# A graph kernel's edge tables: the source's one-hot factored into a row of 128 and a tile

## The chip, the cores and the metric

The kernel runs on one core of a Trainium2 chip. The time is that of the device, in microseconds (us), as the median of three runs. A profile is one further execution with the hardware profiler on.

## What is computed

A graph with 1250 nodes and 21250 edges, sorted by destination; node features are 1250 x 512 in f32. Four layers of attention along the edges with a small MLP each, then one weighted aggregation along the same edges:

```
scores = einsum('ehd,ehd->eh', q[src], k[dst]);  attn = softmax of scores over the edges of each src
out    = segment_sum(attn * v[dst], src)                       # 4 layers, 4 heads
msgs   = x[dst] * edge_weight[:, None]
x      = layernorm(x + segment_sum(msgs, src) @ weight.T)      # last step
```

The kernel replaces the sparse steps by dense ones. It first makes two tables of 1250 x 1250: how often an edge goes from node s to node d (its logarithm is added to dense scores), and the sum of the edge weights for each such pair (the matrix of the last step).

## The kernel before

The stage that matters is the making of the two tables (CW, 128 rows x 2 tables x 10 source tiles x 1250 destinations, f32 in SBUF). The source node is the row: node s lies in tile s // 128, row s % 128. Edges are cut into 56 groups (NG) of 3 x 128 (GK = 3 blocks b); an edge of a block is one row of the matmul's contraction. As the edges are sorted by destination, all of a group lie in a window of 28 destinations (WIN) that begins at a base read from a table. If a group broke that rule, a general path would be taken by a flag; it isn't here.

For each group n:

- VectorE (sources, L1054) and ScalarE (L797) make one-hots of the edges' source over all 1280 places: VectorE one block of three, and a second in one group of four, in bf16; ScalarE the others in fp8.
- VectorE (window, L1047) compares the destination's offset with 28 places, for four groups at once (a chunk); GpSimd (weigh, L611) multiplies that mask with three bf16 parts of the edge weight. This gives 4 x 28 = 112 columns per block: a count and three weight parts.
- TensorE (L1575 to L1581) makes 10 tiles x 3 blocks = 30 matmuls, the one-hot of 128 sources as the loaded operand, the 112 columns as the moving one, into three PSUM banks; groups alternate between two sets of banks.
- VectorE (groups, L1075) adds four slices of 10 x 28 into CW: the counts, and one after the other the three weight parts.

The order in each engine is written out by hand. One-hots are made three groups ahead (AHEAD = 3, four buffers). TensorE's group n waits for VectorE's additions of group n-2. In between, each engine does other early work at fixed groups: on VectorE the angles of the conditioning (before group 8), residuals of rows (before groups 16 and 24) and statistics of x (before group 48); on ScalarE sines, SiLU and casts; on TensorE the conditioning's matmuls. Before the first group a plan is made: the edge lists are loaded as 56 x 384, cast by ScalarE (L740, L742), reduced to each group's base on VectorE (L1014 to L1018), turned by TensorE (turn_edges, L1506) and copied to eT (L1021). The semaphore eplan tells that it is there. At the same time GpSimd, ScalarE and the DMA queue fill CW with zeros. The stage ends with the memset at L1161 (tables_done); the layers wait for it.

Of the kernel before, what the change touches and what calls it, by code (L numbers as in the profile page):

```python
# [46 lines left out]
SLOT = 128  # L47
CHUNK_G = 4
NCH = NG // CHUNK_G
SBUFS = 4  # L50
AHEAD = SBUFS - 1
UNROLL_G = 2 * CHUNK_G
# [34 lines left out]

BOTH = 0
# [52 lines left out]
def build(nc, T, out):  # L141
    ctx = ExitStack()
    with ctx:
# [79 lines left out]
        with ExitStack() as prep:  # L223
            rest_of_weights = sb("rest_of_weights", [P, V_HEAD], F32, prep)
            with ExitStack() as load:
                iota_i = sb("iota_i", [P, NP], I32, load)
                src_i = sb("src_i", [NG, GE], I32, load)
                dst_i = sb("dst_i", [NG, GE], I32, load)
                ef = sb("ef", [NG, 4, GE], F32, load)
                gcol = sb("gcol", [NG, 2], F32, load)  # L230
            with ExitStack() as full:
                oh_src = sb("oh_src", [P, P], BF16, full)
                oh_dst = sb("oh_dst", [P, 4, N], BF16, full)
            onehot = sb("onehot", [P, SBUFS, 2, NP], BF16, prep)
            oh8 = sb("oh8", [P, SBUFS, 2, NP], F8, prep)
# [14 lines left out]
        with ExitStack() as start_of_layer:  # L250
            wv_hi = sb("wv_hi", [P, KT, D], F32R, start_of_layer)
            with ExitStack() as prep:
                wv_raw = sb("wv_raw", [P, KT, D], F32, prep)
            wv_lo = sb("wv_lo", [P, KT, D], F32R, start_of_layer)
            with ExitStack() as prep:
                eT = sb("eT", [P, 4, GK, NG], F32, prep)
                wpart = sb("wpart", [P, 3, NG, GK], BF16, prep)
# [10 lines left out]
        with ExitStack() as prep:  # L268
            wres = sb("wres", [P, GK, NG], F32, prep)
            win = sb("win", [P, 2, CHUNK_G * GK, 4, WIN], BF16, prep)  # L270
# [34 lines left out]
        e_win, e_parts, e_onehot, e_sum, e_count, e_chain = (sem(n) for n in ("e_win", "e_parts", "e_onehot", "e_sum", "e_count", "e_chain"))  # L305
# [16 lines left out]
        counted_groups = [e_sum, e_chain, e_count, g_chain, a_onehot]  # L322
# [229 lines left out]
        def _(pool):  # L552
# [55 lines left out]
            between = {8: (cond_rest,), 10: (last_x,)}  # L608

            pool.wait_ge(eplan, 2)  # L610
            def weigh(c, lo, hi):  # L611
                for part in range(3):
                    oh = win[:, c % 2, lo * GK:hi * GK, 0, :].rearrange("p (g b) w -> p g b w", b=GK)
                    o = win[:, c % 2, lo * GK:hi * GK, 1 + part, :].rearrange("p (g b) w -> p g b w", b=GK)
                    wp = wpart[:, part, c * CHUNK_G + lo:c * CHUNK_G + hi, :]
                    m = pool.tensor_tensor(o, oh, wp.unsqueeze(3).to_broadcast([P, hi - lo, GK, WIN]), ALU.mult)
                m.then_inc(e_parts, 1)

            pool.wait_ge(e_win, 1)
            weigh(0, 0, 1)  # L620
            weigh(0, 1, CHUNK_G)
            flag = pool.value_load(grow_i[0:1, NG:NG + 1], min_val=0, max_val=1)
            for c in range(NCH):
                if c:
                    with pool.If(flag < 1):
                        pool.wait_ge(e_win, c + 1)
                        weigh(c, 0, CHUNK_G)
                        pool.wait_ge(e_parts, c + 2)
                for work in between.get(c, ()):
                    work()  # L630
# [101 lines left out]
        def _(act):  # L732
# [58 lines left out]
            with act.If(flag < 1):  # L791
                for n in range(NG):
# [205 lines left out]
        def _(dve):  # L998
# [13 lines left out]

            dve.wait_ge(dst_cast, 1)
# [3 lines left out]
            dve.wait_ge(off_made, 1)  # L1017
            dve.tensor_reduce(gcol[:, 1:2], ef[:, 1, :], AX.X, ALU.max).then_inc(off_made, 1)  # L1018
# [12 lines left out]
            turned(0, 0)  # L1031
            link(dve.tensor_tensor(wres[:], weight, parts[0], ALU.subtract))
            link(dve.tensor_copy(parts[1], wres[:]))
            dve.wait_ge(edges_turned, 3)
            turned(1, 2)
            link(dve.tensor_tensor(wres[:], wres[:], parts[1], ALU.subtract))
            dve.tensor_copy(grow[:].rearrange("o k g -> o (k g)"), ps[0:1, 2 * 512 + cols:2 * 512 + cols + 2 * NG])
            link(dve.tensor_copy(parts[2], wres[:]))
            dve.tensor_scalar(near[:], eT[:, 0, :, 0:NG], -STEP, NEAR, ALU.mult, ALU.add)
            turned(2, 3).then_inc(eplan, 1)  # L1040
# [6 lines left out]
            def window(c, first):  # L1047
                off = eT[:, 1, :, first].rearrange("p b g -> p g b")
                dve.tensor_tensor(win[:, c, :, 0, :].rearrange("p (g b) w -> p g b w", b=GK),
                                  iota_h[:, 0:WIN].unsqueeze(1).unsqueeze(1).to_broadcast([P, CHUNK_G, GK, WIN]),  # L1050
                                  off.unsqueeze(3).to_broadcast([P, CHUNK_G, GK, WIN]), ALU.is_equal)\
                   .then_inc(e_win, 1)

            def sources(j, b, group):  # L1054
                m = dve.tensor_scalar(onehot[:, j % SBUFS, b, :], iota_h[:], eT[:, 0, b, group], HOT, ALU.is_equal, ALU.mult)  # L1055
                if b == (1 if j % CHUNK_G == BOTH else 0):
                    m.then_inc(e_onehot, 1)

            window(0, slice(0, CHUNK_G))
# [15 lines left out]
            def groups(i):  # L1075
                for j in range(UNROLL_G):
                    dve.wait_ge(e_sum, START + i * UNROLL_G + j + 1)
                    base = dve.value_load(grow_i[0:1, bass.ds(i * UNROLL_G + j, 1)], min_val=0, max_val=N - WIN)  # L1078
                    sums = ps[:, (j % 2) * 3 * 512:(j % 2) * 3 * 512 + NT * SLOT].rearrange("p (t s) -> p t s", s=SLOT)
                    sums = sums[:, :, 0:4 * WIN].rearrange("p t (k w) -> p k t w", k=4)  # L1080
                    counts = CW[:, 0, :, bass.ds(base, WIN)]
                    weights = CW[:, 1, :, bass.ds(base, WIN)]
                    at = START + i * 3 * UNROLL_G + 3 * j
                    ahead = bass.ds(i * UNROLL_G + j + AHEAD, 1)
                    dve.wait_ge(e_chain, at)
                    dve.tensor_tensor(weights, weights, sums[:, 1], ALU.add).then_inc(e_chain, 1)  # L1086
                    dve.wait_ge(e_count, START + i * UNROLL_G + j)
                    dve.tensor_tensor(counts, counts, sums[:, 0], ALU.add).then_inc(e_count, 1)  # L1088
                    dve.wait_ge(e_chain, at + 1)
                    dve.tensor_tensor(weights, weights, sums[:, 2], ALU.add).then_inc(e_chain, 1)  # L1090
                    if i * UNROLL_G + j + AHEAD < NG:
                        sources(j + AHEAD, 0, ahead)
                    dve.wait_ge(e_chain, at + 2)
                    dve.tensor_tensor(weights, weights, sums[:, 3], ALU.add).then_inc(e_chain, 1)  # L1094
                    if i * UNROLL_G + j + AHEAD < NG:
                        if (j + AHEAD) % CHUNK_G == BOTH:
                            sources(j + AHEAD, 1, ahead)
                    if j == 0:
                        window(1, bass.ds(i * UNROLL_G + CHUNK_G, CHUNK_G))
                    if j == CHUNK_G and (i + 1) * UNROLL_G < NG:  # L1100
                        window(0, bass.ds(i * UNROLL_G + UNROLL_G, CHUNK_G))
# [34 lines left out]
            with dve.If(flag < 1):  # L1136
                groups(NG // UNROLL_G - 1)
                dve.wait_ge(e_chain, START + 3 * NG)
                dve.wait_ge(e_count, START + NG)
# [352 lines left out]
        def _(pe):  # L1492
# [21 lines left out]
            pe.wait_ge(src_cast, 1)  # L1514
            turn_edges(0, 0).then_inc(edges_turned, 1)
            pe.wait_ge(dst_cast, 1)
            turn_edges(2, 3)
            pe.wait_ge(off_made, 1)
            turn_edges(1, 2)
            pe.wait_ge(off_made, 2)  # L1520
# [3 lines left out]
            m.then_inc(edges_turned, 1)  # L1524

# [36 lines left out]
            for n in range(NG):  # L1562
                for work in between.get(n, ()):
                    work()
                with pe.If(flag < 1):
                    c, gl = divmod(n, CHUNK_G)
                    if gl == 0:
                        pe.wait_ge(e_parts, c + (2 if c else 1))
                    elif n == 1:
                        pe.wait_ge(e_parts, 2)  # L1570
                    pe.wait_ge(e_onehot, n + 1)
                    pe.wait_ge(a_onehot, START + n + 1)
                    pe.wait_ge(e_chain, START + 3 * (n - 1))
# [399 lines left out]
```

## Time and profile before

| | us |
|---|---|
| median of 3 runs | 1860.27 |
| lowest and highest | 1858.53, 1863.58 |
| the profiled execution | 1858.52 |
| its span in the profile | 1856.7 |

The profile's page gives each engine's busy time, and the span in 40 slices of 46.4 us, each digit a tenth of busy time. The table stage is in the first four slices.

```profile
PE 1745.5 (94%) x11805; PEld 1500.2 (81%) x11805; DVE 1245.1 (67%) x2366; ACT 908.2 (49%) x1468; POOL 432.3 (23%) x545
PE   4766999999999999999999999999999999999998
DVE  7898865675856567668665665677557657675844
ACT  9996454454542445445433554455335446453221
POOL 3233130010381301001743010005621001036201
PEclk9998999999999999999999999999999999999899
```

PE is TensorE's matmuls, PEld its loads of the left operand, DVE VectorE, ACT ScalarE, POOL GpSimd. PEclk is the granted clock of TensorE in tenths of full speed. L1494 is the helper through which all matmuls go.

### The profile page before, as it was taken

To read this page: it belongs to the slowest core of one execution; us is meant where nothing else is said; L and a number is where in the kernel's file an instruction comes from. 1 tells how busy PE (TensorE), PEld (TensorE's weight loads), DVE (VectorE), ACT (ScalarE), POOL (GpSimd) and SP (SyncE) were. 2 spreads that over 40 slices of the span, in tenths; PEclk is the share of its full clock that TensorE was granted. 3 is DMA by queue.
4 is the path that set the end of the run, shared out by engine and by line. 5 is a ranking of instruction groups with operands and counts; after the bars stand their busy time and mean duration, and the time that the engine had idled before them with its cause. 6 is when DMAs were issued, how large, how long until landed. Compare 5 with 4: busy or idle time off the path is not lost.

```text
span 1856.7 us, 30729 instructions
## 1 busy us (share of the span) xinstructions
PE 1745.5 (94%) x11805; PEld 1500.2 (81%) x11805; DVE 1245.1 (67%) x2366; ACT 908.2 (49%) x1468; POOL 432.3 (23%) x545
## 2 busy tenths in 40 slices
PE   4766999999999999999999999999999999999998
PEld 4665778888887888888888888887888888879777
DVE  7898865675856567668665665677557657675844
ACT  9996454454542445445433554455335446453221
POOL 3233130010381301001743010005621001036201
PEclk9998999999999999999999999999999999999899
DMA  3041552242310324224201332332114224241121
GB/s 126 2 130 69 209 160 89 95 129 89 114 39 22 105 76 142 95 75 132 67 23 59 108 125 81 106 116 75 35 30 131 87 82 146 85 139 43 42 89 64
DMA packets 63885, 168.62 MB, mean 91 GB/s; under 512 B 5957, under 2 KB 24250, under 8 KB 63735
## 3 DMA queue, kind: packets, MB, share of 16 engines
q10 hardware_dynamic: 23040, 102.41, 16.9%
q1 hardware_dynamic: 40700, 64.25, 10.8%
q8 instruction: 95, 1.56, 0.3%
q14 instruction: 50, 0.41, 0.1%
HBM read 145.04 MB, written 16.99 MB: 87 GB/s over the span
## 4 chain that ended last, share of the span: by engine, by line
PE 79%; DVE 10%; issue 4%; ACT 2%; DMA 1%; POOL 1%; DVEq 1%; SPq 0%; ACTq 0%; POOLq 0%
PE ps L1494 68%; PE ps L1716 9%; PE ps L1635 2%; DVE onehot L1055 1%; DVE prob L1248 1%; DVE CW L1088 1%; DVE PT_lo L1264 1%; DVE CW L1090 1%; DVE CW L1094 1%; POOL x L657 1%; DVE CW L1086 1%; ACT PT_hi L865 1%; DMA piece<-in_L_gnn_m_w_dram 1%; PE ps L1933 1%; DVEq L1078 0%
## 5 line engine op out<-in xcount | busy, mean ns | idle before, releaser
L865 ACT ACTIVATE PT_hi<-ps 128x512 fp32r<-128x512 f32 x400 | 238.4, 596 | 246.3 <-PE ps L1716 246.1
L1264 DVE TENSOR_TENSOR PT_lo<-ps,PT_hi 128x512 fp32r<-128x512 f32 x400 | 274.4, 687 | 49.8 <-ACT PT_hi L865 42.3
L847 ACT ACTIVATE prob<-prob,nmax 128x1250 f32<-128x1250 f32 x160 | 214.2, 1339 | 136.8 <-DVE nmax L1248 136.8
L1716 PE MATMUL ps<-ident,prob 128*128 128x128 f32 x1600 | 248.2, 278 | 12.2 <-DVE PT_lo L1264 12.0
L1248 DVE CUSTOM_DVE_ANT_0 prob<-ps,Lr 128x1250 f32<-128x1250 f32 x160 | 232.4, 1452 | 31.9 <-PE ps L1494 30.6
L1716 PEld LDWEIGHTS ps<-ident,prob 128*128 128x128 f32 x1600 | 181.9, 140 | 78.7 <-DVE PT_lo L1264 61.5
L1494 PE MATMUL ps<-PT_hi,v_hi 128*128 128x256 f32 x800 | 228.2, 285 | 1.2 <-DVE PT_lo L1264 1.2
L1494 PE MATMUL ps<-PT_lo,v_hi 128*128 128x256 f32 x800 | 226.1, 283 | 0.0
L1494 PE MATMUL ps<-PT_hi,v_lo 128*128 128x256 f32 x800 | 225.6, 282 | 0.0
L1494 PE MATMUL ps<-yT,wqk_hi 128*128 128x512 f32 (+1 forms) x768 | 213.0, 364 | 0.0
L1494 PE MATMUL ps<-k_hi,q_hi 128*128 128x512 f32 (+2 forms) x480 | 191.8, 400 | 0.5
L1494 PE MATMUL ps<-k_hi,q_lo 128*128 128x512 f32 (+2 forms) x480 | 169.7, 353 | 0.0
L1494 PE MATMUL ps<-k_lo,q_hi 128*128 128x512 f32 (+2 forms) x480 | 169.5, 353 | 0.0
L653 POOL TENSOR_TENSOR wo_lo<-piece,wo_hi 128x512 fp32r<-128x512 f32 x16 | 20.4, 1273 | 613.8 <-ACT wo_hi L896 613.8
L1494 PEld LDWEIGHTS ps<-PT_hi,v_hi 128*128 128x128 f32 x800 | 152.4, 191 | 2.5 <-issue 2.0
L1494 PEld LDWEIGHTS ps<-PT_lo,v_hi 128*128 128x128 f32 x800 | 152.7, 191 | 0.1
L1494 PEld LDWEIGHTS ps<-PT_hi,v_lo 128*128 128x128 f32 x800 | 152.6, 191 | 0.0
L1278 DVE SCALAR_TENSOR_TENSOR x<-ps,rnorm,x 128x512 f32<-128x512 f32 x160 | 119.3, 746 | 47.2 <-PE ps L1494 47.2
L1494 PE MATMUL ps<-win,onehot 128*128 128x112 bf16 x700 | 94.1, 222 | 59.3 <-DVE CW L1094 46.1
L1494 PEld LDWEIGHTS ps<-yT,wqk_hi 128*128 128x128 f32 x768 | 132.1, 189 | 19.2
L1494 PE MATMUL ps<-yT,wqk_lo 128*128 128x512 f32 (+1 forms) x384 | 137.1, 357 | 0.0
L797 ACT ACTIVATE oh<-iota_h,near 128x1280 fp8e4<-128x1280 f16 x98 | 125.1, 1350 | 7.7 <-PE ps L1494 7.6
(210 smaller groups left out, 3790.9 us busy)
## 6 DMA issues: line engine op xcount, KB each, us to landing
Lr<-l_table ACTq DMA_DIRECT2D x160, 625.0 KB, 3.9
piece<-in_L_gnn_m_w_dram SPq DMA_DIRECT2D x32, 256.0 KB, 2.7
w_table<-CW SPq DMA_DIRECT2D x5, 1250.0 KB, 8.2
prob<-w_table SPq DMA_DIRECT2D x10, 625.0 KB, 4.0
x<-in_x_dram SPq DMA_DIRECT2D x2, 2304.0 KB
CW<-CW SPq DMA_DIRECT2D x7, 625.0 KB
piece<-in_L_gnn_wo_dram SPq DMA_DIRECT2D x16, 256.0 KB, 4.8
piece<-in_L_gnn_wq_dram SPq DMA_DIRECT2D x15, 256.0 KB, 2.8
```

The costliest lines, as they stand in the source:

```text
L653: pool.tensor_tensor(lo, raw, hi.bitcast(F32), ALU.subtract).then_inc(S["piece_split"], 1)
L657: pool.tensor_tensor(x[:, t, :], x[:, t, :], bo_rows[:], ALU.add).then_inc(S["bo_added"], 1)
L797: m = act.activation(oh8[:, n % SBUFS, b - 1, :], iota_h[:], ACT.Abs_reciprocal_sqrt, bias=near[:, b, n:n + 1], scale=STEP, saturate=False)
L847: act.activation(buf, buf, ACT.Exp, bias=nmax[:, i % 4:i % 4 + 1], scale=-1.0, accum_out=prob[:, i % 3, N:N + 1]).then_inc(S["exped"], 1)
L865: act.activation(o, i, ACT.Copy).then_inc(S["pt_hi"], 1)
L1055: m = dve.tensor_scalar(onehot[:, j % SBUFS, b, :], iota_h[:], eT[:, 0, b, group], HOT, ALU.is_equal, ALU.mult)
L1248: dve.tensor_tensor_reduce(prob[:, i % 3, 0:N], ps[:, off:off + N], Lr[:, i % LBUFS, :], -1.0, BIG, ALU.add, ALU.min, nmax[:, i % 4:i % 4 ...
L1264: dve.tensor_tensor(lo, i, hi.bitcast(F32), ALU.subtract).then_inc(S["pt_split"], 1)
L1278: dve.scalar_tensor_tensor(out=x[:, t, :], in0=bank(wo_bank(h, t)), scalar=rnorm[:, i % 8:i % 8 + 1], in1=x[:, t, :], op0=ALU.mult, op1=AL ...
L1494: return pe.matmul(o, a, b, start=start, stop=stop)
L1635: m = pe.transpose(bank(5 + n % 2, k * P, (k + 1) * P), y[:, k * P:(k + 1) * P], ident[:])
L1716: m = pe.transpose(bank(5 + n % 2, at * P, (at + 1) * P), prob[:, (NT * h + 2 * g + j) % 3, d * P:(d + 1) * P], ident[:])
```

## The change

The source's one-hot over 1280 places is split into two factors. A node's row (s % 128) becomes a one-hot of 128, made four times per block on VectorE: plain, and times the weight, the weight's remainder after its first bf16 part, and the remainder after two (each rounded to bf16 as it is written). These are the loaded operands (left). The node's tile and the destination's offset become one place, tile x 28 + offset, of 280; its one-hot is made by ScalarE in fp8 for all three blocks (right), and is the moving operand. TensorE makes 12 matmuls of 280 columns into two banks per group. VectorE adds both tables in one operation. GpSimd's products, the window masks and the semaphores e_win, e_parts and e_count go. The tile is found by scaling and rounding in the plan (rows_made), the place is made after the offsets. The wpart, source and destination copies, needed by the general path alone, come after the first three groups' rows. Buffers are laid out anew: ef has 6 parts, iota_i, src_i and others no longer share memory with the general path's.

```diff
 @@ VectorE, the plan @@
+            dve.wait_ge(src_cast, 1)
+            link(dve.tensor_scalar(ef[:, 5, :], ef[:, 0, :], 1.0 / P, -(P - 1.0) / (2 * P), ALU.mult, ALU.add))
+            link(dve.tensor_scalar(ef[:, 5, :], ef[:, 5, :], MAGIC, None, ALU.add))
+            link(dve.tensor_scalar(ef[:, 5, :], ef[:, 5, :], -MAGIC, None, ALU.add))
+            dve.scalar_tensor_tensor(out=ef[:, 4, :], in0=ef[:, 5, :], scalar=-float(P), in1=ef[:, 0, :], op0=ALU.mult, op1=ALU.add)\
+               .then_inc(rows_made, 1)
             dve.wait_ge(dst_cast, 1)
...
             dve.wait_ge(off_made, 1)
+            dve.wait_ge(rows_made, 1)
+            dve.scalar_tensor_tensor(out=ef[:, 5, :], in0=ef[:, 5, :], scalar=float(WIN), in1=ef[:, 1, :], op0=ALU.mult, op1=ALU.add)\
+               .then_inc(off_made, 1)
...
-            def sources(j, b, group):
-                m = dve.tensor_scalar(onehot[:, j % SBUFS, b, :], iota_h[:], eT[:, 0, b, group], HOT, ALU.is_equal, ALU.mult)
...
+            def rows(j, group):
+                for b in range(GK):
+                    for part in range(4):
+                        weight = (None, eT[:, 3, b, group], wres[:, 0, b, group], wres[:, 1, b, group])[part]
+                        m = dve.tensor_scalar(left[:, j % SBUFS, b, part, :], iota_h[:, 0:P], eT[:, 4, b, group], weight,
+                                              ALU.is_equal, ALU.mult if part else ALU.bypass)
+                m.then_inc(e_onehot, 1)
+
             for j in range(AHEAD):
-                for b in range(2 if j % CHUNK_G == BOTH else 1):
-                    sources(j, b, slice(j, j + 1))
+                rows(j, slice(j, j + 1))
+            dve.wait_ge(edges_turned, 4)
+            turned(0, 4)
+            turned(2, 5)
+            dve.tensor_copy(parts[2], wres[:, 1])
...
 @@ VectorE, one group @@
-                    dve.tensor_tensor(weights, weights, sums[:, 1], ALU.add).then_inc(e_chain, 1)
...
-                    dve.tensor_tensor(counts, counts, sums[:, 0], ALU.add).then_inc(e_count, 1)
...
+                    sums = ps[:, (j % 2) * 1024:(j % 2) * 1024 + 1024].rearrange("p (k s) -> p k s", k=2)[:, :, 0:PLACES]
+                    both = CW[:, :, :, bass.ds(base, WIN)]
+                    dve.wait_ge(e_chain, START + i * UNROLL_G + j)
+                    dve.tensor_tensor(both, both, sums.rearrange("p k (t w) -> p k t w", w=WIN), ALU.add).then_inc(e_chain, 1)
                     if i * UNROLL_G + j + AHEAD < NG:
+                        rows(j + AHEAD, bass.ds(i * UNROLL_G + j + AHEAD, 1))
 @@ ScalarE @@
-                    for b in (2,) if n % CHUNK_G == BOTH else (1, 2):
-                        m = act.activation(oh8[:, n % SBUFS, b - 1, :], iota_h[:], ACT.Abs_reciprocal_sqrt, bias=near[:, b, n:n + 1], scale=STEP,
-                                           saturate=False)
+                    for b in range(GK):
+                        m = act.activation(right[:, n % SBUFS, b, :], iota_h[:, 0:PLACES], ACT.Abs_reciprocal_sqrt, bias=near[:, b, n:n + 1],
+                                           scale=STEP, saturate=False)
 @@ TensorE @@
+                    if n >= 2:
+                        pe.wait_ge(e_chain, START + n - 1)
+                    at = (n % 2) * 1024
+                    for b in range(GK):
+                        for part in range(4):
+                            o = ps[:, at:at + PLACES] if part == 0 else ps[:, at + 512:at + 512 + PLACES]
+                            m = mm(o, left[:, n % SBUFS, b, part, :], right[:, n % SBUFS, b, :],
+                                   b == 0 and part < 2, b == GK - 1 and part in (0, 3))
```

## Rows read from the trace of the kernel before

**Rows 1.** Busy time by stage: stretch, length, busy us of each engine, clock, DMA share, GB/s.

```profile
21.24:177.01 155.77, 103.00 (x1703) 93.88 (x1700) 139.30 (x326) 138.25 (x119) 38.28 (x56) 0.95 0.17 44
```

**Rows 2.** Groups by line: op, shapes, count, busy us, mean ns, idle before.

```profile
L797 ACT ACTIVATE oh<-iota_h,near 128x1280 fp8e4<-128x1280 f16 x98 | 125.1, 1350 | 7.7 <-PE ps L1494 7.6
L1055 DVE TENSOR_SCALAR onehot<-iota_h,eT 128x1280 bf16<-128x1280 f16 x70 | 44.1, 634 | 0.0
L1086 DVE TENSOR_TENSOR CW<-CW,ps 128x280 f32 x56 | 24.8, 443 | 21.7 <-PE ps L1494 12.1 <-DVE CW L1094 8.0 <-issue 1.4
L1264 DVE TENSOR_TENSOR PT_lo<-ps,PT_hi 128x512 fp32r<-128x512 f32 x400 | 274.4, 687 | 49.8 <-ACT PT_hi L865 42.3
```

**Rows 3.** Waits from 21 to 177 us: total us, times, longest.

```profile
PE ps L1494 <- DVE CW L1094: 46.8, 44, 7.2
DVE CW L1086 <- PE ps L1494: 12.1, 5, 6.5
DVE CW L1086 <- DVE CW L1094: 8.0, 22, 0.7
```

**Rows 4.** Tensor_scalar by line and shape; the last gives minimum, median, maximum in ns.

```profile
L1111 DVE TENSOR_SCALAR sin_b<-sin_b 128x640 f32<-128x640 f32 x1 | 0.5, 495 | 0.0
L1110 DVE TENSOR_SCALAR sin_b<-sin_b,fcol 128x640 f32<-128x640 f32 x1 | 0.6, 553 | 0.0
L1468 DVE TENSOR_SCALAR res<-x,mv,rs 128x512 f32<-128x512 f32 x10 | 5.5, 547 | 9.9 <-POOL rs L728 9.9
L1039 DVE TENSOR_SCALAR near<-eT 128x168 f32<-128x168 f32 x1 | 0.2, 249 | 0.0
L1055 DVE TENSOR_SCALAR onehot<-iota_h,eT x70: 541/547/901, 12.6 to 169.0; 128x1280 bf16<-128x1280 f16 x70
```

**Rows 5.** VectorE in order of time: start, duration in us, line, idle before.

```profile
24.62 0.90 DVE L1055 TENSOR_SCALAR onehot<-iota_h,eT 128x1280 bf16<-128x1280 f16 x1
...
60.57 0.45 DVE L1086 TENSOR_TENSOR CW<-CW,ps 128x280 f32 x1 [0.35 <-issue]
...
61.65 0.55 DVE L1055 TENSOR_SCALAR onehot<-iota_h,eT 128x1280 bf16<-128x1280 f16 x1
62.11 0.44 DVE L1094 TENSOR_TENSOR CW<-CW,ps 128x280 f32 x1
```

**Rows 6.** VectorE in order of time, in the last part.

```profile
1736.36 0.51 DVE L1430 TENSOR_SCALAR x<-x,mv,rs 128x512 f32<-128x512 f32 x1
1736.79 0.68 DVE L1425 TENSOR_TENSOR x<-x 128x512 f32<-128x512 f32 x1
```

**Rows 7.** The chain that ended last, TensorE's first group.

```profile
17.48 2.97 PE ps L1494 x30
```

**Rows 8.** VectorE in order of time, around the other work in the stage.

```profile
40.23 0.15 DVE L1107 TENSOR_SCALAR fcol<-fcol_i 128x1 f32<-128x1 int32 x1
...
47.21 0.45 DVE L1086 TENSOR_TENSOR CW<-CW,ps 128x280 f32 x1 [0.37 <-issue]
...
67.12 2.28 DVE L1120 TENSOR_TENSOR row_raw<-row_raw,row_part 69x2048 f32<-69x2048 f32 x1
...
152.25 0.69 DVE L1071 BATCH_NORM_STATS2 bn<-x 128x6 f32<-128x512 f32 x1
...
157.00 0.45 DVE L1086 TENSOR_TENSOR CW<-CW,ps 128x280 f32 x1 [0.67 <-issue]
...
177.01 0.06 DVE L1161 MEMSET viol<- 1x1 f32 x1 [0.62 <-DVE CW L1094]
```

**Rows 9.** VectorE and ScalarE in order of time, at the start.

```profile
6.32 1.16 DVE L1016 TENSOR_SCALAR ef<-ef,gcol 56x384 f32<-56x384 f32 x1
...
12.57 2.15 DVE L1055 TENSOR_SCALAR onehot<-iota_h,eT 128x1280 bf16<-128x1280 f16 x4
14.62 1.28 ACT L797 ACT_TABLE_LOAD   x1
21.24 0.45 DVE L1086 TENSOR_TENSOR CW<-CW,ps 128x280 f32 x1 [6.52 <-PE ps L1494]
```

More of the change, by code:

```diff
@@ L46 @@
 WIN = 28
-SLOT = 128
-CHUNK_G = 4
-NCH = NG // CHUNK_G
+PLACES = NT * WIN
 SBUFS = 4
 AHEAD = SBUFS - 1
-UNROLL_G = 2 * CHUNK_G
+UNROLL_G = 8
 ET = NG * GK
@@ L86 @@
 HALF = NP // 2
-BOTH = 0
 HOT = 2.0 ** -6
@@ L225, in build @@
             with ExitStack() as load:
[L226 to L235, printed above, removed]
+                oh_src = sb("oh_src", [P, P], BF16, load)
+                oh_dst = sb("oh_dst", [P, 4, N], BF16, load)
+            iota_i = sb("iota_i", [P, NP], I32, prep)
+            src_i = sb("src_i", [NG, GE], I32, prep)
+            dst_i = sb("dst_i", [NG, GE], I32, prep)
+            ef = sb("ef", [NG, 6, GE], F32, prep)
+            gcol = sb("gcol", [NG, 2], F32, prep)
+            left = sb("left", [P, SBUFS, GK, 4, P], BF16, prep)
             grow = sb("grow", [1, 2, NG], F32, prep)
@@ L268, in build @@
         with ExitStack() as prep:
-            wres = sb("wres", [P, GK, NG], F32, prep)
-            win = sb("win", [P, 2, CHUNK_G * GK, 4, WIN], BF16, prep)
+            wres = sb("wres", [P, 2, GK, NG], F32, prep)
+            wpart = sb("wpart", [P, 3, NG, GK], BF16, prep)
+            right = sb("right", [P, SBUFS, GK, PLACES], F8, prep)
+            after_right = sb("after_right", [P, 80], F32, prep)
             after_y1 = sb("after_y1", [P, 24], F32, prep)
@@ L304, in build @@
         a_onehot = sem("a_onehot")
-        e_win, e_parts, e_onehot, e_sum, e_count, e_chain = (sem(n) for n in ("e_win", "e_parts", "e_onehot", "e_sum", "e_count", "e_chain"))
+        e_onehot, e_sum, e_chain, rows_made = (sem(n) for n in ("e_onehot", "e_sum", "e_chain", "rows_made"))
         g_chain, g_onehot, g_sum = (sem(n) for n in ("g_chain", "g_onehot", "g_sum"))
@@ L606, in last_x @@
                 pool.memset(x[:, NT - 1, :], 0.0).then_inc(f_set, 1)
[L608 to L630, printed above, removed]
+            cond_rest()
+            last_x()
             pool.wait_ge(bias_copied, 1)
@@ L1030, in _ @@
             dve.wait_ge(edges_turned, 2)
-            turned(0, 0)
-            link(dve.tensor_tensor(wres[:], weight, parts[0], ALU.subtract))
-            link(dve.tensor_copy(parts[1], wres[:]))
+            turned(4, 0)
+            link(dve.tensor_tensor(wres[:, 0], weight, parts[0], ALU.subtract))
+            link(dve.tensor_copy(parts[1], wres[:, 0]))
+            link(dve.tensor_tensor(wres[:, 1], wres[:, 0], parts[1], ALU.subtract))
             dve.wait_ge(edges_turned, 3)
[L1035 to L1040, printed above, removed]
+            link(turned(5, 2))
+            dve.tensor_scalar(near[:], eT[:, 5, :, 0:NG], -STEP, NEAR, ALU.mult, ALU.add).then_inc(eplan, 1)
+            link(dve.tensor_copy(grow[:].rearrange("o k g -> o (k g)"), ps[0:1, 2 * 512 + cols:2 * 512 + cols + 2 * NG]))
             link(dve.tensor_reduce(viol[:], grow[:, 1, :], AX.X, ALU.max))
@@ L1078, in groups @@
                     base = dve.value_load(grow_i[0:1, bass.ds(i * UNROLL_G + j, 1)], min_val=0, max_val=N - WIN)
[L1079 to L1085, printed above, removed]
-                    dve.tensor_tensor(weights, weights, sums[:, 1], ALU.add).then_inc(e_chain, 1)
-                    dve.wait_ge(e_count, START + i * UNROLL_G + j)
-                    dve.tensor_tensor(counts, counts, sums[:, 0], ALU.add).then_inc(e_count, 1)
-                    dve.wait_ge(e_chain, at + 1)
-                    dve.tensor_tensor(weights, weights, sums[:, 2], ALU.add).then_inc(e_chain, 1)
-                    if i * UNROLL_G + j + AHEAD < NG:
[L1092 to L1101, printed above, removed]
+                    sums = ps[:, (j % 2) * 1024:(j % 2) * 1024 + 1024].rearrange("p (k s) -> p k s", k=2)[:, :, 0:PLACES]
+                    both = CW[:, :, :, bass.ds(base, WIN)]
+                    dve.wait_ge(e_chain, START + i * UNROLL_G + j)
+                    dve.tensor_tensor(both, both, sums.rearrange("p k (t w) -> p k t w", w=WIN), ALU.add).then_inc(e_chain, 1)
+                    if i * UNROLL_G + j + AHEAD < NG:
+                        rows(j + AHEAD, bass.ds(i * UNROLL_G + j + AHEAD, 1))
             def angles():
@@ L1513, in _ @@
             turn_edges(3, 1).then_inc(edges_turned, 1)
[L1514 to L1520, printed above, removed]
+            pe.wait_ge(rows_made, 1)
+            turn_edges(4, 0).then_inc(edges_turned, 1)
+            pe.wait_ge(off_made, 3)
+            turn_edges(5, 2)
             for i in range(2):
@@ L1524, in _ @@
             m.then_inc(edges_turned, 1)
+            turn_edges(0, 4)
+            turn_edges(2, 5).then_inc(edges_turned, 1)
             def turn_biases():
@@ L1565, in _ @@
                 with pe.If(flag < 1):
[L1566 to L1570, printed above, removed]
                     pe.wait_ge(e_onehot, n + 1)
                     pe.wait_ge(a_onehot, START + n + 1)
-                    pe.wait_ge(e_chain, START + 3 * (n - 1))
-                    pe.wait_ge(e_count, START + n - 1)
-                    for s in range(NT):
-                        for b in range(GK):
-                            at = (n % 2) * 3 * 512 + s * SLOT
-                            by_act = b == 2 or b == 1 and n % CHUNK_G != BOTH
-                            m = mm(ps[:, at:at + 4 * WIN], oh8[:, n % SBUFS, b - 1, nt(s)] if by_act else onehot[:, n % SBUFS, b, nt(s)],
-                                   win[:, c % 2, gl * GK + b].rearrange("p k w -> p (k w)"), b == 0, b == GK - 1)
+                    if n >= 2:
[6 more added lines that the diff above has]
+                                   b == 0 and part < 2, b == GK - 1 and part in (0, 3))
                     m.then_inc(e_sum, 1)
             with pe.If(flag < 1):
-                pe.wait_ge(e_chain, START + 3 * (NG - 1))
-                pe.wait_ge(e_count, START + NG - 1)
+                pe.wait_ge(e_chain, START + NG - 1)
             with pe.Else():
```

17 lines of the change are left out of this document (3 added, 14 removed).

## The prediction

> **What bounds the kernel now.** I read the busy times by stage first, to see where the change can act at all. The table stage runs from the first addition into the tables at 21.24 us to the small memset at 177.01 us that releases the layers; that is 155.77 us, in which VectorE is busy for 139.3 and ScalarE for 138.3, TensorE for 103 at a mean granted clock of 0.95, and GpSimd for 38 [rows 1]. Everything behind it is untouched by the diff, and nothing of it can begin before that memset, so the forecast is the change in length of this stage and in its start.
>
> Next come the groups by line [rows 2]. ScalarE makes 98 one-hot tiles of 1280 columns at 1.35 us each, VectorE 70 at 0.63 us, and VectorE adds four slices of 280 columns for each of the 56 groups, 0.44 us apiece. The reader is to see that neither engine has much idle time: two engines share the bound. The waits say the same [rows 3]: TensorE stands 46.8 us behind VectorE's fourth addition, and VectorE 12.1 us behind TensorE and 8.0 us behind its own chain. So VectorE's 139.3 busy us of 155.8 are the floor of this stage. Relief for ScalarE alone could give back at most the rest, 16.5 us, and only while VectorE's own work does not grow. VectorE's work is therefore what has to be priced.
>
> **What a short VectorE operation costs.** The change replaces long operations with many short ones, so the fixed part decides. Durations first [rows 4]. A tensor_scalar on f32 without a per-partition operand takes 249 ns for 168 columns and 495 for 640: (495-249)/(640-168) = 0.52 ns a column, and 162 ns that do not depend on width. With one per-partition operand the 640 columns take 553 ns: 58 ns for the operand. With two, 512 columns take 547 ns; 162 + 2x58 + 512x0.52 = 544. So each operand is paid for, one after the other. The one-hot of 1280 columns, f16 to bf16 with one operand, has a median of 547 ns; less 162 and 58 leaves 0.256 ns a column, half of what f32 takes.
>
> What counts in a row of operations is not the duration but the spacing of the starts. In the steady stretch the one-hot starts at 61.65 and the next addition at 62.11: 0.46 us for a duration of 0.55, so 0.09 is overlapped [rows 5]. A one-hot of 128 columns with one operand is then spaced by 162 + 58 + 33 - 90 = 0.16 us. With two operands it is 0.22 by the same sum. The one spacing of a two-operand operation that I found gives less: 1736.36 to 1736.79 is 0.43 for 512 columns [rows 6], less 0.266 of streaming plus 0.033 is 0.197. I take 0.205, between the ends 0.197 and 0.22 and nearer to the measured spacing.
>
> **The change, part by part.**
>
> *Rows (VectorE).* Each group gets 12 operations of 128 columns: three with one operand (the plain one-hot) and nine with two (place and weight): 3x0.16 + 9x0.205 = 2.325 us. Three groups are made ahead, 53 in the loop.
>
> *Additions (VectorE).* One of 2x280 columns for four of 280. A tensor_tensor takes 443 ns for 280 columns and 687 for 512, 1.05 ns a column [rows 2]: 443 + 280x1.05 = 737 ns, less 0.09 of overlap 0.65 us. Four cost 4x(0.443-0.09) = 1.41, so this part saves 0.76 us a group. It also ends the chain wait of 8.0 us [rows 3], since 12 operations now lie between two additions.
>
> *Removed from VectorE:* 70 long one-hots (44.1 us busy) and the window masks. Some of the former are slowed while GpSimd weighs the masks, 0.90 us for 0.55 at 24.62 [rows 5]; with GpSimd's products gone (most of its 38 busy us in this stage) I price every short operation undisturbed.
>
> So a group costs VectorE 0.65 + 2.325 = 2.975 us; today the stage has 155.8/56 = 2.78 us a group with everything in it.
>
> *ScalarE.* 168 operations of 280 columns for 98 of 1280. A tile of 1280 takes 1.35 us [rows 2]; one of 280 takes 0.30 if all of that streams and 0.82 if half of it is fixed (0.675 + 0.148), so three take 0.9 to 2.5 us a group, where today 98 tiles are 2.36. Both ends are under VectorE's 2.975; ScalarE drops out of the bound and I cost it at nothing.
>
> *TensorE.* 12 matmuls of 280 columns for 30 of 112: 3360 columns either way. At the low clock the first group takes 2.97 us for its 30 [rows 7], about 0.83 ns a column and 2.8 us for 12; half of that at the full clock. Two groups may be in flight, since the matmuls of group n wait for the addition of n-2, so TensorE has a whole VectorE turn of slack. Cost nothing while VectorE needs more than 2.8 us; below that, the low level would show.
>
> *Between the groups.* Angles 40.23 to 47.21 (6.98 us), twice the residual of the rows (2.28 - 0.09 each), statistics 152.25 to 157.00 (4.75) [rows 8]: 16.1 us on VectorE, unchanged. I leave 2 us for entries of branches (0.67 at 157.00) and for the small conditioning matmuls that hold TensorE once.
>
> *Start.* VectorE gets four operations on 384 columns before the offsets, then one more. Undisturbed they cost some 0.4 to 0.56 us each. The only such operation there, at 6.32, took 1.16 beside GpSimd's filling, and 162 + 58 + 200 = 0.42 alone [rows 9]. The new ones may wait in the same way from 4.9 us. I put the plan's end at about 14.7 us; today the one-hots begin right behind it at 12.57. Today ScalarE is busy filling until its table load at 14.62 [rows 9], which hides the first 1.4 us of that; it would load at about 16, and make its three tiles by 18.7 at about 0.45 each. VectorE's first three groups cost 3x2.325 = 7.0 us instead of 2.15, up to about 22, and two deferred copies and a conversion stand behind them, 0.9 us. The first addition moves from 21.24 to about 23.3, +2.0; the ends are +1 (ScalarE's tiles, then one cold group of TensorE, end at about 22) and +4.
>
> **The sum.** 56x0.65 + 53x2.325 = 36.4 + 123.2 = 159.6 us; + 16.1 + 2.0 + 0.6 for the tail = 178.3. Against 155.8 that is +22.5, with the start +24.5. The profiled execution took 1858.52 us (span 1856.7) and the median of three runs is 1860.27, within 0.1%; the difference is put on the median: 1885. Own range: at 0.197 -3.8, at 0.22 +7.2 (477 two-operand operations in the loop), start 1 to 2 us either way: 1878 to 1895.
>
> **Where a rule speaks.** The rows of both kinds show every per-partition operand paid for [rows 4 to 6]. The Trainium skill, "VectorE: DVE Perf Modes", section "The TRN2 errata", gives VectorE from SBUF 58 cycles and the columns over the mode's factor, with no term for such operands: 94 ns for these 128 columns. It is the first rival below by another road. By that the loop would be 56x0.64 + 53x12x0.094 = 95.7 us and the time about 1821. The same section says that small tiles pay the fixed part each time and advises 512 elements or more, which speaks against this change, and there the trace agrees: 120 to 170 ns of 160 to 205 do not stream.
>
> **The rivals.** *Operands are free in short operations (faster).* If the fetch hides behind the previous operation once that is short, an operation is spaced by 162 + 33 - 90 = 0.105 us: 36.4 + 53x1.26 = 103.2, + 18.7 = 121.9, less 155.8, + 2 is -32: 1828. TensorE carries 1.4 us a group at the full clock, but at the low level its 2.8 us would take VectorE's place, so 1828 also needs the full level. The change turns to a gain once the mean of the twelve is under 0.155 us (153.8 - 36.4 - 18.7, over 636). Against it: 61.65 to 62.11 has its 58 ns although an addition runs before it [rows 5]. Chance 0.06.
>
> *Two operands cost as one (no change).* All twelve at 0.16: 477x0.045 = 21.5 less, +3: 1863. Against it: 547 ns and 0.43 us [rows 4, 6]; for it only that both of these are f32. Chance 0.11.
>
> *The short operations fall a mode lower, or VectorE runs dry at each group (slower still).* At 0.52 ns a column 33 ns more on 636 operations is +21; the load of the group's base with a gap like the 0.35 us before the addition at 60.57 [rows 5], 56 times, is +20: about 1905. Each needs a behaviour that the rows do not show. The Trainium skill, "Advanced Engine Details and Errata", section "Engine Queue Depths", gives VectorE a queue of 8, by which eight short operations would cover that load; no row here shows the depth. Chance 0.15.
>
> *The forecast:* 0.68.
>
> **How the numbers follow.** Range 1872 to 1908: it holds the forecast's own range, the lower mode and part of the way to "no change"; it leaves out the two lower rivals, 0.17. A measurement of this kernel can tell about 0.3% (5.6 us). Slower takes the forecast and the third rival less a little for cases between, 0.81; same 0.11, faster 0.08.
>
> **What would show it.** In the changed profile: the short one-hots with two operands at about 310 ns and spaced by 0.20 to 0.22, those with one at about 250 and 0.16; one addition of 560 columns at 0.74; a turn near 2.97 us without idle VectorE; ScalarE near half busy; the memset at about 201.5 us; and later distances as before. Wrong would be: a spacing under 0.16, VectorE idle behind TensorE, or a tail behind the stage that shrinks.

## The result, and the profile after

| | before | after |
|---|---|---|
| median, us | 1860.19 | 1892.19 |
| lowest and highest, us | 1858.53 to 1863.58 | 1891.56 to 1892.27 |
| span of the profiled execution, us | 1856.7 | 1890.4 |
| first addition into the tables, us | 21.24 | 22.52 |
| end of the table stage, us | 177.01 | 209.71 |
| from there to the end, us | 1679.7 | 1680.7 |

The changed kernel is slower: ratio 1.0173, 95% interval 1.0161 to 1.0185, or +32 us. The forecast was 1885 in 1872 to 1908. In the profile the span grew by 33.7 us: 1.3 before the first addition, 31.4 in the stage (187.19 for 155.77), 1.0 behind it. So the place is the one forecast. The median moved by 32.0 and the profile by 33.7, since the execution of the kernel before that was profiled was one of its faster ones (1858.52 us). The remainder of this document is about why a group costs what it does, and what is won back by asking for it otherwise.

The stage after, busy time by engine, answers to [rows 1] (columns as there: length, TensorE, its loads, VectorE, ScalarE, GpSimd, clock, DMA share, GB/s):

```profile
22.52:209.71 187.19, 102.83 (x714) 69.87 (x712) 183.62 (x717) 89.62 (x181) 9.17 (x17) 0.94 0.13 35
```

VectorE is busy for 183.6 of 187.2 us; ScalarE fell from 138.3 to 89.6, GpSimd from 38.3 to 9.2. TensorE did not move: 102.8 for 103.0, at 0.94 of the clock for 0.95, as 3360 columns a group before and after would have it. The groups by line, answering to [rows 2], and the waits, to [rows 3]:

```profile
L1032 DVE TENSOR_SCALAR left<-iota_h,eT,wres 128x128 bf16<-128x128 f16 x336 | 102.7, 388 | 0.0
L1032 DVE TENSOR_SCALAR left<-iota_h,eT 128x128 bf16<-128x128 f16 x336 | 92.1, 356 | 0.0
L771 ACT ACTIVATE right<-iota_h,near 128x280 fp8e4<-128x280 f16 x168 | 75.6, 517 | 66.7 <-PE ps L1455 66.6
L1061 DVE TENSOR_TENSOR CW<-CW,ps 128x560 f32 x56 | 45.1, 805 | 2.8 <-PE ps L1455 1.6 <-issue 1.0
```

```profile
PE ps L1455 <- DVE CW L1061: 78.4, 48, 8.5
PEld ps L1455 <- DVE left L1032: 74.6, 43, 1.8
ACT right L771 <- PE ps L1455: 66.6, 40, 7.4
DVE CW L1061 <- PE ps L1455: 1.6, 1, 1.6
```

The others wait for VectorE, and VectorE for another engine only once, 1.6 us at the end. One turn of it (from one addition to the next), in order of time, answers to [rows 5]:

```profile
100.73 0.83 DVE L1061 TENSOR_TENSOR CW<-CW,ps 128x560 f32 x1
101.38 0.57 DVE L1032 TENSOR_SCALAR left<-iota_h,eT 128x128 bf16<-128x128 f16 x2
101.76 0.63 DVE L1032 TENSOR_SCALAR left<-iota_h,eT,wres 128x128 bf16<-128x128 f16 x2
102.21 0.57 DVE L1032 TENSOR_SCALAR left<-iota_h,eT 128x128 bf16<-128x128 f16 x2
102.59 0.64 DVE L1032 TENSOR_SCALAR left<-iota_h,eT,wres 128x128 bf16<-128x128 f16 x2
103.03 0.58 DVE L1032 TENSOR_SCALAR left<-iota_h,eT 128x128 bf16<-128x128 f16 x2
103.42 0.64 DVE L1032 TENSOR_SCALAR left<-iota_h,eT,wres 128x128 bf16<-128x128 f16 x2
103.86 0.84 DVE L1061 TENSOR_TENSOR CW<-CW,ps 128x560 f32 x1
```

The starts tell the cost. The addition holds 0.65 us (100.73 to 101.38). A pair of remainders' products (two operands each) holds 0.44 to 0.45, so 0.222 us apiece; a pair of one plain row and the first product (x2 in the lines without wres) holds 0.38, which leaves 0.16 for the plain row. The turn is 3.13 us. TensorE's twelve matmuls of a group, at the low level of its clock (granted 0.50 from 53 to 59 us) and at the full one:

```profile
55.54 2.96 PE L1455 MATMUL ps<-right,left 128*128 128x280 fp8e4 x12 [8.52 <-DVE CW L1061]
61.82 1.59 PE L1455 MATMUL ps<-right,left 128*128 128x280 fp8e4 x12 [1.32 <-DVE CW L1061]
```

The start of VectorE, answering to [rows 9]:

```profile
4.87 1.39 DVE L988 TENSOR_SCALAR ef<-ef 56x384 f32<-56x384 f32 x1 [1.99 <-ACT ef L714]
6.30 1.28 DVE L989 TENSOR_SCALAR ef<-ef 56x384 f32<-56x384 f32 x1
7.62 0.35 DVE L990 TENSOR_SCALAR ef<-ef 56x384 f32<-56x384 f32 x1
...
14.32 0.48 DVE L1032 TENSOR_SCALAR left<-iota_h,eT 128x128 bf16<-128x128 f16 x2
...
22.52 0.76 DVE L1061 TENSOR_TENSOR CW<-CW,ps 128x560 f32 x1
```

### The profile page after: what moved, and what is told of

Read it like the earlier page. It is cut to its first block, busy times and chain, and to the rows that moved or that the text cites. A ratio compares the mean times of both kernels' runs of the same rounds, so it can differ in the third digit from the quotient of the medians.

```text
span 1890.4 us, 29027 instructions
## 1 busy us (share of the span) xinstructions
PE 1747.7 (92%) x10800; PEld 1476.8 (78%) x10800; DVE 1297.4 (69%) x2792; ACT 860.0 (45%) x1538; POOL 399.0 (21%) x500
## 4 chain that ended last, share of the span: by engine, by line
PE 77%; DVE 14%; issue 3%; ACT 2%; DMA 1%; POOL 1%; DVEq 0%; POOLq 0%; ACTq 0%; SPq 0%
PE ps L1455 67%; PE ps L1670 9%; DVE left L1032 7%; DVE CW L1061 2%; PE ps L1589 2%; DVE prob L1209 1%; DVE PT_lo L1225 1%; POOL x L631 1%; ACT PT_hi L839 1%; DMA piece<-in_L_gnn_m_w_dram 1%; PE ps L1887 1%; ACT prob L821 0%; DMA w_table<-CW 0%; DMA l_table<-Lr 0%; POOL mw_lo L627 0%
## 5 line engine op out<-in xcount | busy, mean ns | idle before, releaser
L1455 PE MATMUL ps<-right,left 128*128 128x280 fp8e4 x672 | 97.8, 300 | 89.5 <-DVE CW L1061 78.4
L1455 PEld LDWEIGHTS ps<-right,left 128*128 128x128 bf16 x672 | 65.5, 103 | 121.0 <-DVE left L1032 74.6
```

The costliest lines, as they stand in the source:

```text
L1455: return pe.matmul(o, a, b, start=start, stop=stop)
```

## The experiments

**Without the second operand.**

```diff
-                        weight = (None, eT[:, 3, b, group], wres[:, 0, b, group], wres[:, 1, b, group])[part]
+                        weight = (None, 0.5, 0.5, 0.5)[part]
```

> The changed kernel with a constant in place of the weight in the nine weighted operations of each group, so that none has a second per-partition operand (the second table holds constants in place of weights). Everything else, the counts of operations included, is as in the changed kernel (1892.2 us). Theory (every per-partition operand is paid for, and VectorE alone sets the stage): the spacing of those operations falls from 0.222 to 0.162 us, 477 in the loop give -28.6 us: 1863.5, between 1862 and 1866; the turn falls from 3.13 to 2.59 us. Rival (short operations cost by their number, the operand is hidden): 1892. Rival (TensorE at the low clock, 2.8 us a group, takes over at once): the turn stops at 2.8 us where the clock is low, 1875.

Measured: 1863.8 us (1.0025 of before, 1.0015 to 1.0034), 28.4 under the changed kernel. The second table then holds constants in place of weights. The twelve operations of a group stand in one line now, VectorE in order of time:

```profile
63.28 0.73 DVE L1061 TENSOR_TENSOR CW<-CW,ps 128x560 f32 x1
63.93 2.04 DVE L1032 TENSOR_SCALAR left<-iota_h,eT 128x128 bf16<-128x128 f16 x12
65.88 0.73 DVE L1061 TENSOR_TENSOR CW<-CW,ps 128x560 f32 x1
```

Twelve in 1.95 us are 0.1625 each, and the turn is 2.60. The operand costs 0.06 us although the operations are short, and all of it is on the path: 28.4 us over 477 operations are 0.0595 each. It follows that one reason for the loss is the weight as a per-partition operand; what is left, 1863.8 against 1859.6, is no gain either.

**One part less: nine operations.**

```diff
-                    for part in range(4):
+                    for part in range(3):
                         weight = (None, eT[:, 3, b, group], wres[:, 0, b, group], wres[:, 1, b, group])[part]
...
-                            m = mm(o, left[:, n % SBUFS, b, part, :], right[:, n % SBUFS, b, :],
+                            m = mm(o, left[:, n % SBUFS, b, min(part, 2), :], right[:, n % SBUFS, b, :],
```

> The changed kernel without the third weight part: nine operations a group on VectorE in place of twelve (the second part's matmul runs twice, so TensorE and ScalarE do the same work; the third part of the weight is left out of the second table and the second counted twice). Theory: 159 operations at 0.222 us fewer in the loop, -35.3 us: 1857, between 1855 and 1861, turn 2.47 us. Rival (only what streams and the operands count, the fixed part is overlapped once VectorE is less loaded): 159 x (0.033 + 0.118) = -24: 1868. Rival (TensorE at the low clock takes over): not below 1870.

Measured: 1857.5 us, 34.7 under the changed kernel for 159 operations in the loop: 0.218 us each, the full spacing. It rules out that the fixed part is overlapped. TensorE did not become the bound either, though a group at the low level takes it 2.96 us and the turn is now 2.47: that level held for only part of the stage, whose mean granted clock was 0.93.

**The addition in two.**

```diff
-                    both = CW[:, :, :, bass.ds(base, WIN)]
-                    dve.tensor_tensor(both, both, sums.rearrange("p k (t w) -> p k t w", w=WIN), ALU.add).then_inc(e_chain, 1)
+                    for k in range(2):
+                        table = CW[:, k, :, bass.ds(base, WIN)]
+                        m = dve.tensor_tensor(table, table, sums[:, k].rearrange("p (t w) -> p t w", w=WIN), ALU.add)
+                    m.then_inc(e_chain, 1)
```

> The changed kernel with the addition into both tables made as two of 280 columns, as counts and weights. Theory: two are spaced by 2 x 0.355 = 0.71 us where one takes 0.645, +0.065 x 56 = +3.6 us: 1896, between 1894 and 1898. That prices what the merged addition gave: four of 0.355 to one of 0.645. Rival (the addition hides behind waits): 1892.

Measured: 1895.9 us, +3.7. The merging itself is worth 0.066 us a group. The larger part of what the additions gave, 0.71 us by the spacing of 0.355 for each of the two left out, is that TensorE sums the weight's parts, so that 560 columns are added and not 1120.

**GpSimd's products put back** (as a load without use; the operands are shortened here).

```diff
+            for c in range(NG // 4):
+                with pool.If(flag < 1):
+                    pool.wait_ge(e_sum, START + 4 * c)
+                    for part in range(3):
+                        m = pool.tensor_tensor(masks[:, 1]..., masks[:, 0]..., masks[:, 0, :, 0]..., ALU.mult)
+                        m.then_inc(mask_chain, 1)
```

> The changed kernel with GpSimd's products put back as a load without use: 3 of 336 bf16 columns for every 4 groups, on a tile of zeros of its own. It prices the contention that the change took away. In the kernel before, a long one-hot beside them took 0.90 us for 0.55 and the next 0.68. Theory A (VectorE loses about what it lost there, some 0.5 us in each of 14 chunks): +7 us, 1899. Theory B (the short operations in the quarter-pace mode are held for most of the 2.4 us that GpSimd is busy, since they fill 80% of VectorE's time): +15 to +30 us, 1907 to 1922. No contention: 1892.

Measured: 1911.1 us, +18.9, as the second theory had it. GpSimd, then VectorE, in order of time:

```profile
64.71 2.48 POOL L614 TENSOR_TENSOR masks<-masks 128x336 bf16<-128x336 bf16 x3 [18.97 <-PE ps L1471]
```

```profile
64.41 0.47 DVE L1048 TENSOR_SCALAR left<-iota_h,eT 128x128 bf16<-128x128 f16 x2
64.79 1.63 DVE L1048 TENSOR_SCALAR left<-iota_h,eT,wres 128x128 bf16<-128x128 f16 x2
66.34 0.73 DVE L1077 TENSOR_TENSOR CW<-CW,ps 128x560 f32 x1
```

Two operations that are done in 0.53 us take 1.63 beside GpSimd. In most of the other chunks more than one pair is held, as in the next one, where GpSimd runs from 78.33 to 80.72:

```profile
78.08 1.05 DVE L1048 TENSOR_SCALAR left<-iota_h,eT 128x128 bf16<-128x128 f16 x2
79.05 1.73 DVE L1048 TENSOR_SCALAR left<-iota_h,eT,wres 128x128 bf16<-128x128 f16 x2
```

The first pair starts 0.97 before the second where 0.39 is usual, and the second holds 1.65 where 0.44 is usual: 1.8 us for this chunk, 1.1 for the one before. Over the 13 chunks that lie in it the stage grew from 187.2 to 205.4 us, 1.4 us each, where [rows 5] showed 0.35 on one long one-hot. The first chunk runs ahead of the stage, and the first addition came at 24.07 for 22.52. So the removal of GpSimd's work was not a side effect but a condition: with it in place, this arrangement would cost 51 us and not 32. Only a small part of this was a saving against the kernel before: its 70 long one-hots are busy for 44.1 us [rows 2] where 70 times the median of 547 ns [rows 4] is 38.3, so 5.8 us at most. The Trainium skill, "SBUF — State Buffer", section "Who interferes with whom", says that a VectorE operation in a two-port mode and one of GpSimd lock each other out for a whole instruction. The rows agree in kind: some operations are held by 0.5 us or more while their neighbours keep their spacing, and the addition at 66.34, which reads one of its inputs from PSUM, keeps its 0.73 us beside GpSimd.

**What bounded the kernel before.** In the kernel before, the fourth addition is replaced by a small memset:

```diff
-                    dve.tensor_tensor(weights, weights, sums[:, 3], ALU.add).then_inc(e_chain, 1)
+                    dve.memset(small[:], 0.0).then_inc(e_chain, 1)
```

> The kernel before with the fourth addition of each group (the third weight part, which is then left out of the second table) replaced by a memset of one column, so VectorE has about 56 x 0.30 = 16.5 us less to do, and the others the same. It tests the reading that VectorE and ScalarE share the bound of the stage before. ScalarE needs 98 x 1.26 + 22 = 146 us of the 155.8. Reading right: about half of it comes, 1849 to 1856. Were VectorE alone the bound: 1841 to 1844. Were ScalarE alone: 1859.

Measured: 1849.1 us (0.9952 of before, 0.9937 to 0.9967). With 16.5 us less to do on VectorE, 10.6 came. The stage ends at 167.68, after 146.5 us; in it VectorE is busy for 122.8 and ScalarE for 137.4, so ScalarE now leads. A stretch that runs 2.3 us further says the same:

```profile
21.20:170.00 148.80, 104.09 (x1707) 94.33 (x1706) 124.93 (x330) 139.60 (x121) 40.04 (x58) 0.94 0.19 50
```

VectorE was part of the bound, but not all of it: 5.9 of the 16.5 us did not come. That ScalarE held the rest is read from its busy time; no run took work from ScalarE alone. This is the edge of what was expected (1849 to 1856), nearer to VectorE alone than I had it.

**The nine products as one operation.** The same result as the changed kernel, with another form:

```diff
+            def weigh(j, group):
+                nb = dve_blocks(j)
+                dve.wait_ge(e_plain, j + 1)
+                dve.tensor_tensor(left[:, j % SBUFS, 0:nb, 1:4, :],
+                                  left[:, j % SBUFS, 0:nb, 0, :].unsqueeze(2).to_broadcast([P, nb, 3, P]),
+                                  eT[:, 5:8, 0:nb, group].rearrange("p k b o -> p b k o").to_broadcast([P, nb, 3, P]), ALU.mult)\
+                   .then_inc(e_onehot, 1)
```

with nb = 3 in this version, and the plain rows of group n + 4 made at the end of turn n, where their buffer has just come free.

> The changed kernel computing the same, with the nine weighted operations of a group made as one product on VectorE: the three plain rows, read three times over, times the weight's three parts read along the columns, 1152 columns at the pace of an addition. The plain rows are made one group earlier, so that the product never waits for them. Theory (VectorE's fixed part and operands are the whole loss): 0.064 + 1152/0.96 = 1.264 us in place of 9 x 0.222 = 2.00, turn 0.645 + 3 x 0.16 + 1.264 = 2.39 us; over the loop -39.7 us, the start up to 1.5 earlier: 1851, between 1849 and 1855, which would be under the kernel before (1859.6). Rival (TensorE at the low clock, 2.8 us a group, takes over): not below 1870.

Measured: 1853.3 us (0.9971 of before, 0.9959 to 0.9983). VectorE in order of time:

```profile
63.38 0.73 DVE L1071 TENSOR_TENSOR CW<-CW,ps 128x560 f32 x1
64.03 1.35 DVE L1039 TENSOR_TENSOR left<-left,eT 128x1152 bf16<-128x1152 bf16 x1
65.30 0.57 DVE L1033 TENSOR_SCALAR left<-iota_h,eT 128x128 bf16<-128x128 f16 x3
65.79 0.73 DVE L1071 TENSOR_TENSOR CW<-CW,ps 128x560 f32 x1
```

The product takes 1.04 ns a column (the next run has both 1347 ns for 1152 columns and 946 for 768), where a one-hot takes 0.26: the starts of the same form are spaced by 0.46 us for 1280 columns [rows 5] and by 0.1625 for 128. Yet it holds 1.27 us where nine short operations hold 2.0. The turn is 2.41 us. The start did not follow, where up to 1.5 us had been expected: VectorE was ready at about 21 us and waited 1.8 for its first addition at 22.77.

**ScalarE takes a share.** nb = 2 in three of four groups; in those:

```diff
+                        act.wait_ge(e_plain, n + 1)
+                        for b in range(dve_blocks(n), GK):
+                            for part in range(3):
+                                m = act.activation(left[:, n % SBUFS, b, 1 + part, :], left[:, n % SBUFS, b, 0, :], ACT.Copy,
+                                                   scale=eT[:, 5 + part, b, n:n + 1])
```

> As the one with the products in one, and in three of four groups ScalarE makes the three products of the third block (128 columns each, scale from a per-partition operand), since it has 67 us idle in the stage of the changed kernel. VectorE's product is then 0.064 + 768/0.96 = 0.864 us in those groups: -0.3 us a group on the mean, -16 us: 1836 if VectorE alone sets the stage. ScalarE: 56 x 1.3 + 42 x 3 x 0.3 + 22 of other work = 133 us for a stage of some 131: both near the bound, so 1836 to 1843. Rival (TensorE's low clock level, or the waits among three engines, eat it): 1850 or more.

Measured: 1842.9 us (0.9913 of before, 0.990 to 0.9927), the best of all: 16 us under the kernel before, in the same session (1859.2), and 49 under the changed one. The stage takes 137.46 us from its first addition, VectorE busy for 128.3 and ScalarE for 122.0 in it:

```profile
22.75:160.21 137.46, 101.27 (x716) 70.22 (x714) 128.33 (x288) 121.98 (x304) 6.65 (x17) 0.93 0.18 47
```

**The share in every group**, nb = 2 throughout.

> As the previous one with ScalarE's share in every group. VectorE 4 us less, ScalarE 14 x 0.9 = 12.6 us more: 145 us of ScalarE's work would be the bound of the stage. If ScalarE becomes the bound as the sums say: 1846 to 1852, above the share in three of four. If ScalarE's operations are cheaper than 0.3 us each: not above it.

Measured: 1848.5 us (0.9940 of before). VectorE waited 13.0 us for TensorE, for 5.4 with the share in three of four. ScalarE is busy for 133.2 of the stage's 143.4 us, VectorE for 124.3. The time lies in the range that was expected if ScalarE becomes the bound.

**The groups without a share put beside ScalarE's other work.**

```diff
-            return GK if n % 4 == 0 else GK - 1
+            return GK if n in (8, 9, 13, 14, 15, 17, 18, 19, 21, 22, 31, 32, 39, 46) else GK - 1
```

> As the version with ScalarE's share in three of four groups (1842.9), with the same number of groups without a share (14), but put beside ScalarE's own other work (sines, SiLU, casts of rows) in place of every fourth. In the former VectorE stood 5.4 us behind TensorE, in three places, which in turn waited for ScalarE after its table loads. If those waits are ScalarE's backlog, 2 to 5 us go: 1838 to 1841. If they are the latency of the table loads themselves, nothing: 1843.

Measured: 1846.6 us, 3.7 above the even spread, where 2 to 5 less, or no change, had been expected: a miss, with the wrong sign (the single times overlap a little, 1844.2 to 1847.5 against 1840.7 to 1845.4). VectorE's two longest idle times behind TensorE, of the even spread and then of this one:

```profile
64.51 0.74 DVE L1077 TENSOR_TENSOR CW<-CW,ps 128x560 f32 x1 [2.10 <-PE ps L1475]
90.09 0.74 DVE L1077 TENSOR_TENSOR CW<-CW,ps 128x560 f32 x1 [2.26 <-PE ps L1475]
```

```profile
67.39 0.74 DVE L1077 TENSOR_TENSOR CW<-CW,ps 128x560 f32 x1 [3.24 <-PE ps L1475]
95.64 0.74 DVE L1077 TENSOR_TENSOR CW<-CW,ps 128x560 f32 x1 [4.12 <-PE ps L1475]
```

The same two waits are there and have grown by 3.0 us together, and the first addition comes at 23.65 for 22.75, as group 0 has a share now. The traces tell the two waits apart. Ahead of the first one, TensorE's matmuls of the conditioning wait 3.1 us for ScalarE (1.9 in the even spread), and the 36 matmuls behind them take 6.14 us in both. Ahead of the second one stand 40 small matmuls of the conditioning; they took 6.3 us for 4.9, and TensorE's granted clock was at its low level (0.50) from 88.3 to 95.1 us, where the even spread had it from 85.7 to 89.1. So the second wait grew behind a slower TensorE and not behind ScalarE. Whether the first grew because relief at the disturbed groups comes too late, no run separates; and as the clock's low stretches differ from run to run, the two arrangements may lie closer together than 3.7 us.

## Why the prediction was right, point by point

**The bound.** That VectorE alone would set the stage after is shown by its 183.6 busy us of 187.2 and by the experiments, in which the savings on VectorE arrive nearly in full (28.4 of 28.6 us, 34.7 of 35.3). That it was one part of the bound before is shown by the fewer additions there (10.6 us for 16.5); that ScalarE was the other is argued from its busy time.

**The price of a short operation** was the step on which all rested, and it held in form: a fixed part, a part for each per-partition operand, and about 0.26 ns a column. For one operand 0.16 us was forecast and 0.1625 measured. For two it was 0.205 between ends of 0.197 and 0.22; measured 0.222. This is the term that was mis-sized. It had two sources, a sum of durations (0.22) and one spacing of 0.43 us [rows 6], and the mean of them leaned to the spacing. The sum was right. The spacing was the odd one of its line (L1430): that operation lasted 0.51 us and its nine neighbours of the same line 0.53 to 0.54, and it was not the only one to be found. Seven microseconds earlier the trace of the kernel before has

```profile
1729.07 0.54 DVE L1430 TENSOR_SCALAR x<-x,mv,rs 128x512 f32<-128x512 f32 x1
1729.52 0.69 DVE L1425 TENSOR_TENSOR x<-x 128x512 f32<-128x512 f32 x1
```

and the same again at 1732.24 and 1732.69: 0.45 us, which by the prediction's own step (less 0.266, plus 0.033) gives 0.217. The difference, 0.017 on 477 operations, is 8.1 us. The experiment without the second operand gives the operand itself: 0.060, for the 0.058 from [rows 4]. With 0.22 the forecast would have been 1892.

**The addition.** 0.65 forecast, 0.65 measured.

**The other terms.** The sum gave 178.3 us for the stage; 187.2 came: 56 x 0.645 + 53 x 2.484 = 167.8 for the loop (159.6 forecast), and 19.4 for the rest (18.7). The first addition came at 22.52, not 23.3. The plan's end was put at 14.7 us and was at about 14.3; the first two new operations took 1.39 and 1.28 us beside GpSimd's filling, as feared, the third 0.35. Behind the stage 1.0 us came that no step names; in the experiments and versions this distance lies between 1678.7 and 1680.4 us and follows nothing that I varied.

**TensorE and ScalarE at nothing.** Held. ScalarE's tile of 280 columns took 517 ns, between the bounds of 0.30 and 0.82. TensorE took the same time as before. But its price was low: 2.97 us for 3360 columns [rows 7] is 0.88 ns a column and not 0.83, and a group at the low level took 2.96 us, not 2.8 (1.59 at the full one, not 1.4). That is under the measured turn of 3.13, and level with the turn of 2.975 that was forecast. In the runs with turns of 2.60 us and less the low level came for 3 to 10 us at a time and was mostly hidden: with the products in one, TensorE took 6.87 us for 36 matmuls from 49.84 while VectorE kept its turn of 2.40. Not always, though: in each of these six runs VectorE waited once behind the conditioning's matmuls, for 1.2 to 4.1 us at 90 to 98 us, with the clock low then or just before. The three versions with a share for ScalarE waited another 2.1 to 6.9 us at 64 to 70 us, with the clock low again and a wait for ScalarE ahead of it. What part of these waits is the clock's is not separated, and no run had the low level for the whole stage.

**The rivals.** Free operands: excluded by the first experiment (1863.8, not 1892), and with it the time of 1821 by the cycle table of the Trainium skill's "VectorE: DVE Perf Modes", section "The TRN2 errata". Its 58 cycles and the columns over four are 94 ns, where the trace has 162 with one operand and 222 with two; less 0.06 for each operand, 102 remain by this extrapolation (no short one-hot without such an operand was run), so the table's form is near and the operands are what it lacks. Two operands for one: excluded by the same run. A lower mode: 0.1625 us for 128 columns is the prediction's sum with 33 ns of streaming; with 66 it would have been 0.196. VectorE dry at each group: the trace has 1.0 us of such idle time in all, in two places. That the short operations run undisturbed once GpSimd's products are gone was no rival but a premise, taken without a test; the fourth experiment shows what stood behind it, 18.9 us.

## What to carry to other kernels

Factoring a one-hot cut the columns that VectorE writes, but those cost only 0.26 ns each, and 12 operations a group of 0.16 to 0.22 us each took their place: count operations and per-partition operands ahead of columns. Where many short operations differ only in a scalar, one tensor_tensor that reads each input several times over (with stride zero) does their work in one, at a quarter of the pace and still faster (1.27 for 2.0 us). And when an edit frees an engine that was near the bound, share the work anew: that was worth another 10 us here.

## What the runs showed of the hardware that was not expected

A short VectorE operation's duration in the profile is not its cost. In the changed kernel the same operation lasts from 302 to 526 ns while the starts keep their 0.222 us; the durations creep up over stretches of the loop and fall back behind other work, and in the run with the two additions the median of the same form is 318 ns for 378, at the same spacing. The first line is the changed kernel, the second the one with two additions (minimum, median, maximum in ns):

```profile
L1032 DVE TENSOR_SCALAR left<-iota_h,eT,wres x336: 302/378/526, 14.7 to 205.2; 128x128 bf16<-128x128 f16 x168
```

```profile
L1032 DVE TENSOR_SCALAR left<-iota_h,eT,wres x336: 300/318/747, 14.7 to 209.3; 128x128 bf16<-128x128 f16 x168
```

What makes them creep is open. The other surprise is the size of GpSimd's hold on short operations: 1.4 us for each 2.4 to 2.5 us of its work.
